# Attention values as the stationary operand, the softmax's division ahead of the transposes, and squares added before the norm matmuls

## What is computed

```
q, k, v = split(x @ Wqkv)                       # 16 heads of 64
q = l2norm(q) * qs;  k = l2norm(k) * ksc        # norm over the 64 of a head
q = q * cos * scale + rotate_half(q) * sin * scale      # k likewise, with 1 / scale
sim = einsum('bhwie,bhwje->bhwij', bq, bk2) * 8.0       # 32 queries, 64 keys: own window and the one before
attn = softmax(where(mask, -max, sim), -1)
out = einsum('bhwij,bhwje->bhwie', attn, bv2)
x = out.reshape(b, n, 1024) @ Wo + x
x = a * gelu(gate) @ W2 + b2 + x                # after layer norm and W1, tokens shifted by one in half of the channels
```

## Time and profile before

| | us |
|---|---|
| median of 3 runs (3630.65 to 3669.45) | 3644.95 |
| the profiled execution | 3633.57 |
| its span, first to last instruction | 3631.4 |
| TensorE busy | 3440.9 |
| ScalarE busy | 2701.4 |
| VectorE busy | 2676.7 |
| GpSimd busy | 1059.2 |

### The profile page before, as it was taken

How to read it: one execution, slowest core, us unless ns; L and a number is a source line. 1 busy time by engine, 2 the same in 40 slices (tenths; PEclk the granted TensorE clock), 3 DMA queues, 4 the chain that set the end, 5 groups by cost and what they waited for, 6 DMA issues and landing times.

```text
span 3631.4 us, 155395 instructions
## 1 busy us (share of the span) xinstructions
PE 3440.9 (95%) x64764; PEld 2500.4 (69%) x64764; DVE 2676.7 (74%) x5333; ACT 2701.4 (74%) x9033; POOL 1059.2 (29%) x892
## 2 busy tenths in 40 slices
PE   7789999999999999999999999999999999999997
PEld 4457667776776767676677767666766776677775
DVE  5667777777777777777777777777777776777775
ACT  5668787777877777777778777777777786877776
POOL 2223233332323233232323223232323232332321
PEclk9899999999999999999999999999999999999999
DMA  2065655655565555555465655555565655555563
GB/s 69 1 129 112 130 114 123 135 112 123 125 129 108 123 130 117 127 114 125 105 147 112 138 111 118 118 129 118 112 138 107 133 123 124 109 120 120 111 130 76
DMA packets 361283, 421.61 MB, mean 116 GB/s; under 512 B 52291, under 2 KB 265814, under 8 KB 359814
## 3 DMA queue, kind: packets, MB, share of 16 engines
q1 hardware_dynamic: 360582, 411.67, 52.5%
HBM read 19.30 MB, written 2.10 MB: 6 GB/s over the span
## 4 chain that ended last, share of the span: by engine, by line
PE 77%; SPq 8%; issue 4%; DMA 3%; POOL 1%; DVE 1%; ACT 1%; POOLq 0%; DVEq 0%; ACTq 0%
PE ring_ps L1231 19%; PE out_ps L1341 9%; SPq L475 8%; PE ring_ps L1276 7%; PE score_ps L1294 7%; PE out_ps L1370 6%; PE out_ps L1330 6%; PE small_ps L1242 5%; PE ring_ps L1314 4%; PE ring_ps L1305 4%; DMA kt<-ks 3%; PE ring_ps L1377 3%; PE score_ps L1286 2%; POOL qs L606 1%; PE ring_ps L1266 1%
## 5 line engine op out<-in xcount | busy, mean ns | idle before, releaser
L764 ACT ACTIVATE probs<-score_ps,neg_max,rq 128x64 f32<-128x64 f32 x3072 | 1202.5, 426 | 331.2 <-DVE neg_max L1021 329.9
L606 POOL TENSOR_TENSOR ks<-prod 128x1024 f32<-128x1024 f32 x192 | 454.6, 2368 | 2305.3 <-DVE prod L983 2305.3
L983 DVE TENSOR_TENSOR prod<-ring_ps,tables 128x512 f32<-128x512 f32 x1536 | 952.8, 683 | 134.4 <-PE ring_ps L1231 130.1
L1231 PE MATMUL ring_ps<-xs,wqk 128*128 128x256 f32 x3072 | 776.4, 391 | 22.9 <-issue 14.8
L764 ACT ACTIVATION_READ_ACCUMULATOR probs<-score_ps,neg_max,rq 128x1 f32 x3072 | 699.9, 228 | 0.0
L1231 PEld LDWEIGHTS ring_ps<-xs,wqk 128*128 128x128 f32 x3072 | 562.4, 192 | 148.9 <-issue 60.0
L719 ACT ACTIVATE square<-ring_ps,biases 128x512 f32<-128x512 f32 x768 | 503.3, 702 | 39.1 <-DVE prod L983 28.1
L752 ACT ACTIVATE att_t<-ring_ps 128x512 f32<-128x512 f32 x384 | 219.4, 596 | 375.1 <-PE ring_ps L1314 375.0
L606 POOL TENSOR_TENSOR qs<-prod 128x1024 f32<-128x1024 f32 x192 | 452.6, 2357 | 16.7 <-DVE prod L983 12.7
L1016 DVE TENSOR_REDUCE row_max<-score_ps 128x8 f32<-128x512 f32 x384 | 246.5, 684 | 242.5 <-PE score_ps L1294 242.5
L1276 PE MATMUL ring_ps<-wv,xs 128*128 128x512 f32 x768 | 414.8, 622 | 0.6 <-issue 0.5
(11 more groups left out here) (184 smaller groups left out, 4188.2 us busy)
## 6 DMA issues: line engine op xcount, KB each, us to landing
v<-vs SPq DMA_DIRECT2D x1344, 128.0 KB
qt<-qs SPq DMA_DIRECT2D x768, 128.0 KB
kt<-ks SPq DMA_DIRECT2D x768, 128.0 KB
v<-vs SPq DMA_DIRECT2D x192, 64.0 KB
wqk<-in_L_ffn_Wqkv SPq DMA_DIRECT2D x6, 1024.0 KB, 5.2
wv<-in_L_ffn_Wqkv SPq DMA_DIRECT2D x6, 512.0 KB, 4.9
wo<-in_L_ffn_Wo SPq DMA_DIRECT2D x6, 512.0 KB
out_dram<-ks SPq DMA_DIRECT2D x16, 128.0 KB, 1.9
```

Source lines behind the costliest of these rows:

```text
L606: pool.tensor_tensor(dst, prod_a[p % 2], prod_b[p % 2], ALU.add).then_inc(rot_ready, 1)
L764: last = nc.scalar.activation(probs[i][:, j, e, :], score_ps[e][:, KEYS * j:KEYS * (j + 1)], ACT.Exp, bias=neg_max[:, h:h + 1], scale=rq[p ...
L983: last = V.tensor_tensor((prod_b if a else prod_a)[p % 2][:, f, :] .rearrange("p (u c) -> p u c", u=2), bank[:, :].rearrange("p (u c) -> p ...
L1231: last = mm(bank_of(s)[:, TOKENS * f:TOKENS * (f + 1)], wqk[:, n, 2 * c + f, a, :], xs[:, WINDOW:PADDED], start=True, stop=True)
```

## The change

Three things are done, and the orders of four engines are written anew.

1. `PV` takes the values as the stationary operand (64 keys x 64 channels) and moves `pt` (32 columns). The result comes out with channels on the partitions, as `WO` needs it, so the turn `O` and the copy through a ring bank go: `OC` reads `out_ps` directly. Even pairs write `out_ps[0]`, odd ones `out_ps[1]`, each of the two key halves to a side of 64 partitions; the odd pairs' sides are swapped, and the host lays out Wo to match. Tile 1's values wait until `OC` has copied tile 0's.
2. The division moves ahead of the turn: `AN` replaces `AT` and scales half a tile's probs in place, in four steps per batch. `T` waits for it.
3. GpSimd adds the squares of both halves (`ZK0`, `ZK1`, `ZQ0`, `ZQ1`); `NK` and `NQ` then take 4 matmuls instead of 8.

`PAD` stands for an unused turn of the ring of three banks. Some small tiles of the start now share memory with others. In the new file line 1323 is `PV`, 1242 the norms, 1040 and 1043 `AN`, 600 the added squares, 613 `AD`, 989 the products, 1022 and 1027 `M`, 1005 `KM`.

```diff
 PE_ORDER = """
-S00 S01 PA0 PB0 PA1 BI WO PB1 PA2 CEN PB2 VAR NK PA3 UP0 TK PB3 S10 S11 UP1 UP2 TU T00 T01 KN0 NQ V0 KN1 V1 PV00
-PV01 T10 V2 TQ V3 T11 O00 PV10 PV11 O01 DN O10 O11
+PA0 PB0 S00 S01 PA1 PB1 BI WO PA2 PB2 CEN NK PA3 VAR PB3 TK S10 UP0 S11 UP1 V0 UP2 TU T00 KN0 KN1 NQ V1 PV00 DN
+T01 V2 T10 PV01 V3 PAD TQ T11 PV10 PV11
 """
 DVE_ORDER = """
-XS M0 RB0 RA0 RA1 BI XA XB RB1 RA2 RB2 XG CK RA3 RB3 H0 M1 UC TC00 TC01 KM0 H1 H2 CQ KM1 VC1 TC10 AT0 VC3 TC11
-AT1 X
+XS RA0 RB0 M0 RA1 RB1 BI XA RA2 XB RB2 CK RA3 XG RB3 AN00 AN01 H0 M1 UC H1 TC00 H2 KM0 KM1 VC1 AN10 X TC01 CQ
+TC10 AN11 VC3 TC11
 """
 ACT_ORDER = """
-E00 E01 QA0 QB0 E02 QA1 SQ QB1 LN QA2 E03 RTK LG G0 QB3 QB2 QA3 G1 G2 LE E10 E11 VC0 E12 E13 VC2 RTQ OC00 OC01
-OC10 OC11
+QA0 QB0 E00 E01 QA1 QB1 E02 QA2 SQ E03 LN RTK QB2 QA3 LG G0 QB3 VC0 G1 G2 LE E10 E11 E12 E13 VC2 OC00 OC01 OC10
+OC11 RTQ
 """
 POOL_ORDER = """
-AD0 AD1 AD2 RK AD3 TB
+AD0 ZK0 ZK1 AD1 AD2 RK AD3 TB ZQ0 ZQ1
 """
...
-RING = [s for s in PE_ORDER if s[0] in ("PA", "PB", "TU", "KN", "V", "T", "O", "DN")]
+RING = [s for s in PE_ORDER if s[0] in ("PA", "PB", "TU", "KN", "V", "T", "DN", "PAD")]
...
+        sq_sum = [sb(f"sq_sum{i}", [P, 2 * TOKENS]) for i in range(COUPLES)]
...
+                if kind in ("ZK", "ZQ"):
+                    n, c = int(kind == "ZQ"), s[1]
+                    p = COUPLES * n + c
+                    last_square = max(rank(ACT_ORDER, (x, p), "QA", "QB") for x in ("QA", "QB"))
+                    pool.wait_ge(sq_ready, at(g, QK_BANKS, last_square + 1))
+                    pool.wait_ge(norm_made, at(g, 2, n))
+                    pool.tensor_tensor(sq_sum[c][:, :], square[c][0][:, :], square[c][1][:, :], ALU.add
+                                       ).then_inc(sq_added, 1)
...
-                    act.wait_ge(norm_made, at(g, 2, n))
+                    act.wait_ge(sq_added, at(g, 2 * COUPLES, 2 * n + p % COUPLES + 1 - COUPLES))
...
                 if kind == "OC":
                     i, c = s[1], s[2]
-                    act.wait_ge(o_made, at(g, 2 * TILES, 2 * i + c + 1))
+                    act.wait_ge(pv_ready, at(g, TILES, i + 1))
                     if i == 0 and c == 0:
                         act.wait_ge(wo_ready, at(g, 1))
-                    nc.scalar.activation(att_t[:, 4 * c:4 * c + 4, P * i:P * (i + 1)],
-                                         bank_of(("O", i, c))[:, :].rearrange("p (j c) -> p j c", c=P), ACT.Copy
+                    nc.scalar.activation(att_t[:, :, P * i:P * (i + 1)].rearrange("p (j a) q -> p a j q", a=2)[:, c, :, :],
+                                         out_ps[c][:, :].rearrange("p (j c) -> p j c", c=P), ACT.Copy
                                          ).then_inc(o_copied, 1)
...
-                        act.wait_ge(inv_ready, at(g, TILES))
...
-                if kind == "AT":
-                    i = s[1]
-                    dve.wait_ge(exp_ready, at(g, TILES * PARTS, PARTS * (i + 1)))
-                    V.reciprocal(inv_sums[i][:, :, :].rearrange("p j e -> p (j e)"), sums[i][:, :]
+                if kind == "AN":
+                    i, c = s[1], s[2]
+                    part = slice(4 * c, 4 * c + 4)
+                    dve.wait_ge(exp_ready, at(g, TILES * PARTS, PARTS * i + 2 * (c + 1)))
+                    V.reciprocal(inv_sums[i][:, part, :].rearrange("p j e -> p (j e)"), sums[i][:, 8 * c:8 * c + 8]
                                  ).then_inc(inv_ready, 1)
-                    dve.wait_ge(inv_ready, at(g, TILES, i + 1))
-                    dve.wait_ge(pv_ready, at(g, TILES, i + 1))
-                    for e in range(2):
-                        last = V.tensor_tensor(
-                            att[i][:, :, e, :], out_ps[e][:, :].rearrange("p (j d) -> p j d", d=DIM_HEAD),
-                            inv_sums[i][:, :, e:e + 1].to_broadcast([P, PAIRS, DIM_HEAD]), ALU.mult)
-                    last.then_inc(att_ready, 1)
+                    dve.wait_ge(inv_ready, at(g, 2 * TILES, 2 * i + c + 1))
+                    V.tensor_tensor(probs[i][:, part, :, :].rearrange("p j e k -> p (j e) k"),
+                                    probs[i][:, part, :, :].rearrange("p j e k -> p (j e) k"),
+                                    inv_sums[i][:, part, :].rearrange("p j (e o) -> p (j e) o", o=1)
+                                    .to_broadcast([P, PAIRS, KEYS]), ALU.mult).then_inc(scaled, 1)
...
-                    last_square = max(rank(ACT_ORDER, (x, COUPLES * n + c), "QA", "QB")
-                                      for x in ("QA", "QB") for c in range(COUPLES))
-                    pe.wait_ge(sq_ready, at(g, QK_BANKS, last_square + 1))
+                    pe.wait_ge(sq_added, at(g, 2 * COUPLES, COUPLES * (n + 1)))
                     pe.wait_ge(norms_ready, at(g, 2, n))
-                    for a in range(2):
-                        for u in range(QUADS):
-                            last = mm(norm2_ps[WINDOW * u:WINDOW * (u + 1), :], head_ones[:, :],
-                                      square[u // 2][a][:, TOKENS * (u % 2):TOKENS * (u % 2 + 1)],
-                                      start=(a == 0), stop=(a == 1), skip_group_check=True)
+                    for u in range(QUADS):
+                        last = mm(norm2_ps[WINDOW * u:WINDOW * (u + 1), :], head_ones[:, :],
+                                  sq_sum[u // 2][:, TOKENS * (u % 2):TOKENS * (u % 2 + 1)],
+                                  start=True, stop=True, skip_group_check=True)
                     last.then_inc(norm_made, 1)
...
-                    pe.wait_ge(exp_ready, at(g, TILES * PARTS, PARTS * i + 2 * (c + 1)))
+                    pe.wait_ge(scaled, at(g, 2 * TILES, 2 * i + c + 1))
...
-                if kind == "O":
+                if kind == "PV":
                     i, c = s[1], s[2]
-                    bank_free(g, s)
-                    if c == 0:
-                        pe.wait_ge(att_ready, at(g, TILES, i + 1))
-                    for j in range(4):
-                        last = pe.transpose(bank_of(s)[:, P * j:P * (j + 1)],
-                                            att[i][:, 4 * c + j, :, :].rearrange("p e k -> p (e k)"), ident[:, :])
-                    last.then_inc(o_made, 1)
-                if kind == "PV":
-                    i, half = s[1], s[2]
-                    if (i, half) == (0, 0):
+                    if (i, c) == (0, 0):
                         pe.wait_ge(hidden_ready, at(g, FCHUNKS))
                         pe.wait_ge(v_moved, moved(g, 1, V_MOVES))
                         if g == 0:
                             pe.wait_ge(v2_zeroed, 1)
-                    if (i, half) == (1, 0):
-                        pe.wait_ge(att_ready, at(g, TILES, 1))
-                    pe.wait_ge(t_copied, at(g, 2 * TILES, 2 * i + half + 1))
-                    for j in range(PAIRS // 2 * half, PAIRS // 2 * (half + 1)):
+                    if (i, c) == (1, 0):
+                        pe.wait_ge(o_copied, at(g, 2 * TILES, 2))
+                    pe.wait_ge(t_copied, at(g, 2 * TILES, 2 * i + c + 1))
+                    for j0 in range(4 * c, 4 * c + 4, 2):
                         for w in range(WPT):
-                            for e in range(2):
-                                last = mm(out_ps[e][WINDOW * w:WINDOW * (w + 1), DIM_HEAD * j:DIM_HEAD * (j + 1)],
-                                          pt[64 * e:64 * e + 64, j, WINDOW * w:WINDOW * (w + 1)],
-                                          v2[64 * e:64 * e + 64, WPT * i + w,
-                                                     DIM_HEAD * j:DIM_HEAD * (j + 1)],
-                                          start=True, stop=True, skip_group_check=True)
-                    if half == 1:
+                            for j in (j0, j0 + 1):
+                                for e in range(2):
+                                    side, q0 = 64 * (e ^ (j % 2)), P * (j // 2) + WINDOW * w
+                                    last = mm(out_ps[j % 2][side:side + 64, q0:q0 + WINDOW],
+                                              v2[64 * e:64 * e + 64, WPT * i + w, DIM_HEAD * j:DIM_HEAD * (j + 1)],
+                                              pt[64 * e:64 * e + 64, j, WINDOW * w:WINDOW * (w + 1)],
+                                              start=True, stop=True, skip_group_check=True)
+                    if c == 1:
...
+    wo_parts = np.asarray(laid["L0_ffn_Wo"]).reshape(DEPTH, QUADS, 2, 2, DIM_HEAD, DIM)
+    laid["L0_ffn_Wo"] = np.stack([wo_parts[:, :, 0], wo_parts[:, :, 1, ::-1]], 2).reshape(DEPTH, INNER, DIM)```

How the orders stand, at three places. VectorE, from the last products (`RB3`) to the last scaling of ks (`KM1`), before:

```order
L983 TENSOR_TENSOR prod<-ring_ps,tables 128x512 x4
L1071 SCALAR_TENSOR_TENSOR hidden<-out_ps,b_full,gate 128x256
L1016 TENSOR_REDUCE row_max<-score_ps 128x8 x2
L1021 SCALAR_TENSOR_TENSOR neg_max<-row_max,rq 128x16
L992 COPY rkt<-ring_ps 48x256
L1028 COPY pt<-ring_ps 128x512 x2
```

33 lines of the change are left out of this document (15 added, 18 removed).

## The result

The changed kernel takes **3706.1 us** (median of 4 runs, 3702.85 to 3717.09), the kernel before 3639.8 us beside it (3630.65 to 3669.45): ratio (of the means) 1.0173, 95% interval [1.0109, 1.0237]. It is slower, by between 1.1% and 2.4%. The forecast was 3625 us; 3706 is where rival 1 stood (3720).

A forecast was written before the change was run, and what follows sets the result against it. It took two loops of almost the same length, TensorE's work and the DMA loop, as the bound. The DMA loop stayed; SP's waits for KM1 went (-22 us): 3612, plus 11 for the runs' median, 3625 us; range 3460 to 3780.

The forecast's parts named there:

- rival 1: AD3 on GpSimd gets in ahead of an AN, delaying KM1 to +26.1: +77 us, 3720 us; chance 0.28.
- The exclusion: A VectorE step with two SBUF inputs and a GpSimd step exclude each other; seen as 0.44 against 0.17 us.
- rival 2: No exclusion for large steps: KM1 at +22.8, 2.0 us less per period, 3435 us; chance 0.25.
- If both come ahead of AD3: AN00 and AN01 cost AD3 2 x 0.66 us, so it starts at +16.8 as before, the DMA loop no shorter.
- VectorE asks first: Argument against AD3 getting ahead of AN01, by offsets 0.1 us apart: about +15.9 against +16.0.
- What sets the end: The DMA loop: kt comes late, with TensorE idle before the scores about 2 us in most periods.
- costs TensorE only slack: Halved norm matmuls waiting for GpSimd's sums (ZK1 at +9.3) were no case of their own.
- The row maximum's second step: On VectorE, due at +2.9, it waits for ZK0's end at +3.65: +0.6 us on ScalarE.
- TensorE's work: Per period 34.3 - 2.9 + 0.4 + 0.4, about 32.2 us, with values as weights taken at 3.6 us.
- Norms: Halved norm matmuls on TensorE save 1.1 us per batch, some 0.9 of it time of its own.
- Rival 3: Values' matmuls cost twice as much if two halves cannot write one bank together: +144, 3790 us; chance 0.12.
- The clock: TensorE's waits for kt may often drop its granted clock to 0.50: 0 to +50 us, kept for the range.

The follow-up runs named there:

- e5: Changed kernel with the two-input product of probs and inv_sums replaced by a one-input maximum over the same probs, leaving out the division: 3561.67 us, ratio 0.9787.
- e4: Changed kernel without its third part: eight norm matmuls per step, no sums of squares on GpSimd: 3724.01 us, ratio 1.0242 to the kernel before.
- e3: Changed kernel with both moves, AN01 behind KM1 on VectorE and NQ behind DN on TensorE: 3585.05 us, ratio 0.9857 to the kernel before.
- e1: Changed kernel with AN01 moved from behind AN00 to behind KM1 in VectorE's order: 3609.55 us, ratio 0.9930 to the kernel before.
- e2: Changed kernel with NQ moved behind DN on TensorE, AN01 left in place: 3718.54 us, ratio 1.0232 to the kernel before.
- e8: e3 with one wait added, GpSimd starting AD0 only after tile 0's row maximum: 3548.79 us, ratio 0.9722 to the kernel before.
- e7: e3 without the halved norms: eight norm matmuls per batch, no sums of squares on GpSimd: 3628.13 us, ratio 0.9975 to the kernel before.
- e6: e3 with each half of rows of the values' products writing a bank of its own: 3583.96 us, ratio 0.9844 to the kernel before.

## Why the prediction was wrong, step by step

**The exclusion: right.** It was drawn from one row of 16 elements and priced rival 2 at a quarter. e5 shows it for 128x512, in both directions: VectorE's two-input step holds GpSimd's (0.24 to 0.66 us), GpSimd's holds VectorE's (0.69 to 2.81 us), and a one-input step meets nothing. The Trainium skill (SBUF — State Buffer, section "Who interferes with whom") states it as a lock for the whole instruction; the runs agree, with these numbers.

**The step that failed: "If both come ahead of AD3".** My offsets were close: AN00 at +14.9 (forecast +15.0), AN01 at +15.70 (+15.9), RK's end at +15.65 (+15.4 unstretched, about +16.0 stretched). I took AN00 to stretch RK by 0.6 us; it met only the last of RK's four steps and cost 0.42 us. So AD3 was there first, by 0.09 us in the period shown, and in 92 of 96 periods AN01 was held: 2.81 us in place of 0.66. e4 shows that coming up inside AN00 would not have helped: there AD3 slips in between the two products. The forecast needed AD3 to come up when AN01 had already started. A race decided by less than the error of any of its terms had gone to the forecast because "VectorE asks first". I should have seen that the two cases do not cost alike: AN01 behind AD3 delays H0, M1 and UC, and TensorE through them, AD3 behind AN01 delays the moves by 0.66 us.

**What sets the end: wrong in forecast and in rival 1.** Both had the DMA loop close the period. Rival 1 had the hold right, and its sign (SP waits for KM1 in most periods) came; its 3720 is near 3706, but not by its own sum, and that is luck: it had MK 0.8 us later than before, and MK in fact started at +24.95 (before +25.29), and kt was there 2.8 us before its scores started. KM1 came at +24.96, not at +26.1. One part of that is the wait for ScalarE's gate ahead of H0 when AN01 is not there, as e3's row shows: 0.95 us, in which an AN01 of 0.9 us would have found room; the hold puts H0 off by 1.95 us (rival: 2.35). The larger is M1's second step, which takes 0.76 us where e1 and e3 have 1.00; the rival had it 0.3 us longer. The row of e3:
```profile
1786.47 0.48 DVE L1076 SCALAR_TENSOR_TENSOR hidden<-out_ps,b_full,gate 128x256 f32<-128x256 f32 x1 [0.95 <-ACT gate L794]
```

What grew is the chain AN01, H0, M1, UC, KN0, TensorE's order to PV01, TC10, AN11, T11, the values, PA0, PB0, scores. I had followed H0 and M1 only as far as KM1 and SP, never back to TensorE; the list of what is queued behind a step has to go on until the loop is closed. In the same way PA0 and PB0, moved ahead of the scores, were in my sum only for ScalarE: on TensorE they are 2 us between the values and the scores.

**A term put at nothing: the sums at a change of layer.** I priced the added squares by AD0, ZK0 and ZK1 and said of the norm matmuls' wait that it "costs TensorE only slack". For q that is not so: NQ waits 23.7 us in five periods, because `ZQ0` and `ZQ1` stand behind the tables that GpSimd makes there. e2 and e3, which move NQ, take 29 and 27 us off these five.

**The row maximum's second step: size right, cause wrong.** It takes 0.67 us and ends at +3.76 (medians), against +3.65 forecast with ZK0 as what holds it. All 192 in the changed kernel, to the earlier trace rows:
```profile
L1027 DVE SCALAR_TENSOR_TENSOR neg_max<-row_max,rq x192: 174/752/1204, 205.1 to 3654.2; 128x16 f32<-128x16 f32 x192
```
What holds it is AD0: it does not start at +0.05 but at +1.38, when RB0's product is there, and ZK0 is behind it. e8 shows this on the path: without it the period is 0.4 us shorter.

**TensorE's work: 0.9 us too little.** The forecast's terms without the norms give 34.3 - 2.0 + 0.8 = 33.1 us; e7 has 34.02. Values as weights cost 420.9 against 311.6 us, 17.1 ns per pair and 4.4 us per batch, where I had taken 3.6 between bounds of 3.25 and 5.4. The load took 136 ns for 64 columns, as worked out (28 ns more than 105; it was 31). I had it hidden under its neighbours. That the load is what makes the pair longer is argued, not shown; the four regions in place of eight could do it too, and e6 excludes the bank alone. So the turns gave back little: e7, with the turns gone, AN01 free and NQ moved, is 0.25% faster than before ([0.9955, 0.9995]), far inside the 1% taken as no change.

**Norms: right.** 0.82 us of TensorE's time against 0.9 (e7 and e3), worth 44 us when AN01 is free. In after itself it stands as 3724.01 against 3706.1 us, from separate measurements with intervals that overlap ([1.0217, 1.0268] and [1.0109, 1.0237]), so a gain there is likely, not shown.

**Rival 3: wrong.** The Trainium skill (TensorEngine Tiling (Array Packing), section "Gotcha 1: PSUM Pressure") has row tiles not use the same bank at once; pairs cost 17.1 ns with two halves in one bank and 17.1 ns in two. For this kernel the rule changes nothing.

**Rival 2, its price.** e5 is nearest to a kernel without the large holds: 3562 us, not 3435. I took 2.2 us off the DMA loop, which left 32.6 us, just above my 32.2 us for TensorE. In e5 TensorE has 32.65 us of work in a period and over a microsecond without, and the period is 33.86 us; the five periods at a change of layer are 47 us above five such periods.

**The clock: right at its lower end.** With 2.5 us without work in the period shown the granted clock was 1.00 (2.4 GHz), and over the span 0.986 against 0.988 before.

## What to carry to other kernels

A VectorE step with two SBUF inputs is costly not by its length but by its place: list GpSimd's steps around it, and put it where a collision delays nothing, or make GpSimd, if it has room, wait for it. Moving one word was worth 2.4% and two added waits another 1.9%, more than the arithmetic saved. When two orders are 0.1 us apart, follow both to the end of the loop, and write the program so that the cheap one is certain. And look at the rare periods by themselves: five of 95 held all that e3 gained over e1 and, roughly, half of what the change lost.

## What the runs showed of the hardware

- The hold lasts to the end of the other engine's instruction, and the held one then adds most of its own length: AN01 2.81 us, ending 0.55 us behind a GpSimd step of 2.35 us, against 0.69 us alone. It works in both directions: AD3, behind AN00, takes 2.84 us in place of 2.35 (e4).
- A reduction over 128x512 with one SBUF input ran 384 times in 685 to 687 ns, under GpSimd steps too; so did 1536 products of 128x512 with one input in SBUF and one in PSUM, in 673 to 693 ns.
- A pair of a 64x64 fp32 load and a 32-column stream costs 17.1 ns in four regions, one of a 64x32 load and a 64-column stream 12.7 ns in eight: the same products, 35% dearer with fewer regions and the longer load.
